# Frequency mixing on one core: applying products in four blocks, with the next unit's first building groups between them

## What is computed

```python
Vf = jnp.fft.rfft(phi, n=n, axis=0)
Uf_p = jnp.fft.rfft(u, n=n, axis=1)
Uf_m = jnp.fft.rfft(u * sgn3, n=n, axis=1)
U_plus = jnp.fft.irfft(Vf[None, :, :, None] * Uf_p[:, :, None, :], n=n, axis=1)[:, :sl]
...
out = jnp.einsum('btkd,k,kde->bte', U_plus, s, Mpp)
out = out + jnp.einsum('btkd,k,kde->bte', U_minus, s, Mpm)
```

## Time and profile before

| | us |
|---|---|
| median of 3 runs | 3256.39 |
| the 3 runs | 3248.46, 3256.39, 3266.70 |
| the profiled execution, device time | 3252.43 |
| its span | 3250.7 |
| TensorE busy in the span | 2596.3 (80%) |
| VectorE busy | 1553.5 (48%) |
| ScalarE busy | 1357.3 (42%) |
| GpSimd busy | 267.9 (8%) |

### The profile page before, as it was taken

One profiled execution on the slowest core, in us unless ns is written; L12 is line 12 of the kernel. 1 busy time (PEld: TensorE's weight loads), 2 busy tenths in 40 slices (PEclk: granted clock), 3 DMA queues, 4 the chain that ended last, 5 costly groups with the idle time before them and its releaser, 6 DMA issues. The chain is left out here.

```text
span 3250.7 us, 88750 instructions
## 1 busy us (share of the span) xinstructions
PE 2596.3 (80%) x36720; PEld 2013.4 (62%) x36720; DVE 1553.5 (48%) x3537; ACT 1357.3 (42%) x2728; POOL 267.9 (8%) x493
## 2 busy tenths in 40 slices
PE   0556999455449999989999999999777865899999
PEld 0336888322148888888888888887337621555555
DVE  6441333332425565656555556566112342376666
ACT  0552433254036555656555656565110263233322
POOL 0102111000100000000000000000111001100000
PEclk9776888777779999999999999999995677799999
DMA  7337555333531111111111111110785200000000
GB/s 202 118 96 134 103 96 101 116 129 118 120 96 40 40 41 39 48 40 40 40 40 40 40 40 40 40 40 21 244 285 199 70 0 12 5 21 21 19 20 27
DMA packets 160531, 242.34 MB, mean 75 GB/s; under 512 B 37072, under 2 KB 114691, under 8 KB 156639
## 3 DMA queue, kind: packets, MB, share of 16 engines
q1 hardware_dynamic: 122137, 115.68, 12.9%
q0 software_dynamic: 34048, 102.83, 11.8%
q10 hardware_dynamic: 3969, 18.31, 1.4%
HBM read 145.48 MB, written 91.27 MB: 73 GB/s over the span
## 5 line engine op out<-in xcount | busy, mean ns | idle before, releaser
L962 DVE COPY spc_g<-spc_pz 128x512 f32<-128x512 f32 x1088 | 670.5, 682 | 450.4 <-PE spc_pz L860 450.4
L940 ACT ACTIVATE spc_g<-spc_pz 128x512 f32<-128x512 f32 x1088 | 587.0, 610 | 346.3 <-PE spc_pz L860 344.6
L860 PE MATMUL spc_pz<-spc_v,spc_as 108*128 108x128 bf16 x8704 | 601.0, 222 | 40.5 <-issue 29.7
L860 PEld LDWEIGHTS spc_pz<-spc_v,spc_as 108*128 108x128 bf16 x8704 | 516.6, 99 | 134.7 <-issue 48.0
L878 PE MATMUL spc_pz<-spc_g,spc_u 128*20 128x128 f32 x17408 | 503.8, 274 | 30.0 <-DVE spc_g L962 18.1
L878 PEld LDWEIGHTS spc_pz<-spc_g,spc_u 128*20 128x20 f32 x17408 | 480.3, 133 | 62.6 <-ACT spc_g L940 41.2
L845 PE MATMUL spc_pu<-spc_f,spc_s 128*128 128x256 f32 x816 | 223.6, 399 | 70.9 <-DMA spc_s<-s_sf 70.9
L1591 DVE SCALAR_TENSOR_TENSOR moe_yt<-moe_ex,moe_gb,moe_yt 128x128 f32<-128x128 f32 x768 | 209.7, 343 | 145.8 <-ACT moe_yt L1495 144.7
L1445 PE MATMUL moe_ex<-moe_ew,moe_d 128*128 128x512 f32 x512 | 253.2, 617 | 17.1 <-DVE moe_yt L1591 17.1
L507 DVE SCALAR_TENSOR_TENSOR inv_xo<-inv_pa,inv_mask,inv_xo 128x256 f32<-128x256 f32 x256 | 123.5, 483 | 228.4 <-PE inv_pa L465 173.3
L485 ACT ACTIVATE inv_b<-inv_pb 112x1024 f32<-112x1024 f32 x128 | 125.5, 1022 | 227.6 <-PE inv_pb L444 227.6
(11 more groups left out here) (188 smaller groups left out, 2509.9 us busy)
## 6 DMA issues: line engine op xcount, KB each, us to landing
s_yd<-spc_yo SPq DMA_DIRECT2D x136, 160.0 KB
spc_s<-s_sf POOLq DMA_DIRECT2D x36, 512.0 KB, 6.5
ivs_y<-s_yd POOLq DMA_DIRECT2D x34, 512.0 KB, 5.4
s_td<-ivs_to SPq DMA_DIRECT2D x34, 512.0 KB, 4.7
s_sf<-fwd_so ACTq DMA_DIRECT2D x16, 1024.0 KB, 5.4
bck_t<-s_td POOLq DMA_DIRECT2D x32, 512.0 KB, 3.8
inv_x<-s_xn SPq DMA_DIRECT2D x88, 112.0 KB
inv_x<-s_xn POOLq DMA_DIRECT2D x88, 112.0 KB, 7.6
```

What stands on the lines that cost most here:

```text
L860: m = pe.matmul(pz[:, (p + 2) % 3, e // 4, 2 * FT * (e % 4):2 * FT * (e % 4) + 2 * FT], AS[:, x, 8 * p + e, :], V[:, k, x, :, FT * t:FT * ...
L940: act.activation(g_out(p, 0), g_in(p, 0), ACT.Copy).then_inc(ga, 1)
L962: v.tensor_copy(g_out(p, 1), g_in(p, 1)).then_inc(gd, 1)
```

## The change

Each unit's order on the three engines is written anew. The sixteen building groups of the next unit are no longer all behind the four blocks of applying: group 0 stands behind block 0, groups 1 and 2 behind block 1, groups 3 and 4 behind block 2, the other eleven behind block 3. The engines that copy follow the same order. For this the tile G gets 168 columns instead of 128 for each frequency (EO = 40 more), and plus units use columns 0 to 127, minus units 40 to 167. The groups are taken in an order (`pair_of`) in which the first five write the forty columns that the other unit doesn't read. All blocks of applying use the two banks of one pair (`y_at`), the building groups the others (`PAIR`), and from group 7 on all three pairs. The second step stands behind groups 5, 10 and 15 of the next unit's building. Tokens, their factors and yo become single buffers; GpSimd loads the first tokens and filters ahead of AS.

The core of the diff (sixteen groups of unit 0 are built ahead of the loop; `copy_g`, `copy_y` and `add_y` hold the same operations as before with their waits):

```diff
-        G = A.sb("g", [P, 2 * FT, C])
+        G = A.sb("g", [P, 2 * FT, C + EO])
-        Ss = A.sb("s", [P, 2, 2, NB, 2 * C])
-        F = A.sb("f", [P, 2, 2, 4, NF2])
-        yo = A.sb("yo", [P, 2, FT // 4, C])
+        Ss = A.sb("s", [P, 2, NB, 2 * C])
+        F = A.sb("f", [P, 2, 4, NF2])
+        yo = A.sb("yo", [P, FT // 4, C])
...
         def y_at(h):
-            return pz[:, h // 2, h % 2]
+            return pz[:, 0, h % 2]
+
+        def pair_of(x, j):
+
+            return j if x == 0 else (j + NPR - OWN) % NPR
...
+            load_tokens(0)
+            load_filters(0, 0)
+            for x in range(2):
+                for g, part in enumerate(A_PARTS):
+                    sp.dma_start(AS[KX * g:KX * g + KX, x].rearrange("k e d -> k (e d)"),
+                                 S["AS"][x, part].rearrange("k e d -> k (e d)")).then_inc(as_in, 16)
+            load_filters(1, 1)
...
                     sp.wait_ge(u_done, UB * (f + 1))
-                    load_tokens((f + 2) % NF1, k)
+                    load_tokens(f + 1)
...
+                        make_y(f, k, t, x, 0)
+                        if more:
+                            if end:
+                                pe.wait_ge(in_v[1 - k], 96 * (i + k) + 96)
+                            make_g(nf, nk, nt, nx, 0)
+                        make_y(f, k, t, x, 1)
+                        if more:
+                            make_g(nf, nk, nt, nx, 1)
+                            make_g(nf, nk, nt, nx, 2)
+                        make_y(f, k, t, x, 2)
+                        if more:
+                            make_g(nf, nk, nt, nx, 3)
+                            make_g(nf, nk, nt, nx, 4)
+                        make_y(f, k, t, x, 3)
+                        if more:
+                            for j in range(OWN, NPR):
+                                make_g(nf, nk, nt, nx, j)
+                                if not last and j in STEPS:
+                                    if t == 0 and x == 0 and j == OWN:
+                                        pe.wait_ge(in_s, 48 * (f + 2))
+                                    second_step(f + 1, 1 - k, 3 * (2 * t + x) + STEPS.index(j))
```

More of the change, by code:

```diff
@@ L772, in spectrum @@
     NPR = C // 8
+    OWN = 5
+    EO = 8 * OWN
     UB = 3 * NB
+    NH = FT // 16
+    PAIR = (2, 1, 2, 1, 2, 1, 2, 0, 1, 2, 0, 1, 2, 0, 1, 2)
+    STEPS = (OWN, 10, NPR - 1)
     with Arena(nc, "spc") as A:
@@ L802, in one, with f_loop @@
             return ap[bass.ds(i, 1)].rearrange(f"{' '.join(names)} -> ({names[0]} {names[1]}) {' '.join(names[2:])}")
+        def f_loop(eng, body):
+            with eng.Fori(0, NF1 // 2) as i:
+                for k in range(2):
+                    body(2 * i + k, k, i, False)
+            body(NF1 - 1, 0, NF1 // 2, True)
         @block.gpsimd
         def _(sp):
[L806 to L809, removed]
             def load_filters(f, k):
@@ L851, in make_g @@
                 n = NUN * f + 2 * t + x
[L852 to L864, removed]
@@ L866, in make_y @@
-            def make_y(f, k, t, x):
-                n = NUN * f + 2 * t + x
[L868 to L880, removed]
@@ L883, in _ @@
+            pe.wait_ge(in_s, 48)
             for unit in range(UB):
                 second_step(0, 0, unit)
+            pe.wait_ge(in_v[0], 96)
             pe.wait_ge(as_in, 16 * 12)
+            for j in range(NPR):
+                make_g(0, 0, 0, 0, j)
             def body(f, k, i, last):
-                pe.wait_ge(in_v[k], 96 * (f // 2) + 96 if isinstance(f, int) else 96 * i + 96)
-                if not last:
-                    pe.wait_ge(in_s[1 - k], 48 * i + 48 + 48 * k)
                 for t in range(NTL):
@@ L892, in body @@
                     for x in range(2):
[L893 to L913, removed]
+                        end = x == 1 and t == NTL - 1
+                        if end:
+                            nf, nk, nt, nx = f + 1, 1 - k, 0, 0
+                        else:
+                            nf, nk, nt, nx = f, k, t + x, 1 - x
+                        more = not (end and last)
@@ L954, in _, with copy_g, add_y, body @@
         def _(v):
-            def body(f, k, last):
+            def copy_g(n, x, j):
+                v.wait_ge(g_done, NPR * n + j + 1)
+                v.tensor_copy(g_out(x, j, 1), g_in(j, 1)).then_inc(gd, 1)
+            def add_y(f, t, h):
+                n = NUN * f + 2 * t + 1
+                v.wait_ge(y_done, NH * n + h + 2)
+                v.wait_ge(ya, NH * (NTL * f + t) + h + 1)
+                y = yo[:, 4 * h:4 * h + 4, :].rearrange("p g e -> p (g e)")
+                v.tensor_tensor(y, y_at(h), y, ALU.add).then_inc(yd, 1)
+            for j in range(NPR):
+                copy_g(0, 0, j)
+            def body(f, k, i, last):
                 for t in range(NTL):
```

157 lines of the change are left out of this document (115 added, 42 removed).

## The result

| | before | after |
|---|---|---|
| median, 12 runs each | 3248.28 us | 3264.10 us |
| lowest and highest | 3238.57 to 3266.70 | 3250.13 to 3280.51 |
| profiled execution | 3252.43 us | 3271.32 us |
| its span | 3250.7 us | 3269.6 us |

The ratio is 1.0052, with a 95% interval from 1.0027 to 1.0077: the changed kernel is slower, by 16 us in the medians and by 19 us in the two profiled executions. The forecast was 33 us. The direction was right, the size twice too large. Of all runs in this document one, of a_block (3331.41 us), was slow as a whole at a lower granted clock, and is left out of its median and ratio.

A forecast was written before the change was run, and what follows sets the result against it. No copy engine bounds the stage on average; only TensorE's waits, at most 1.4 of 18.6 us a unit, can be won. Spacing +34.8, U +7.8, start -10 give +32.6: 3289 us; forecast 3273 to 3308, wider range 3252 to 3314.

The forecast's parts named there:

- Waiting taken away: TensorE's waits for copies in a unit fall from 1.41 to 0.98 us: a gain of 0.43 us.
- Changes of shape: Six new passages a unit between applying and building: 3 x 0.19 us towards building, 3 x 0.15 us back.
- The units of before: Unit length before the change, from one pair: 18.56 and 18.70 us, mean 18.63, against 19.15 after.
- The wait for U: Second step now right before the applying products that need its output: +0.49 us, 16 times, +7.8 us.
- The start: Tokens loaded ahead of AS bring the first applying product from 958.95 to 949.0: -10 us (-6 to -14).
- The last units and the returns: All 67 spacings counted at +0.52 us; seven returns of TensorE's loop taken as unchanged, 0, with 3 us each way.
- Single buffers, row spacing: Single token and result buffers stay hidden by 3 us each; G's rows of 672 B instead of 512 B cost 0.
- B: Rival: a change of shape costs nothing where a group stands between two blocks; unit 18.13 us, 3221 us, chance 0.07.
- C: Rival: only the new direction, building to applying, is free; 30 us less, 3259 us, chance 0.11.
- E: Rival: a single buffer's load or result write is late by 6 us, 3 us shown 16 times; 3337 us, chance 0.09.
- D: Rival: loop returns shrink because filter loads no longer run beside the refill; 28 us less, 3261 us, chance 0.07.
- F: Rival: early groups do not overlap, copies or products slow beside applying; +10, 3299 us; forecast with F 0.66.

The follow-up runs named there:

- a_block: The changed kernel with the five early building groups behind the fourth applying block instead of between the blocks: 3301.82 us, ratio 1.0116 to the kernel before.
- b_unroll: The kernel before with TensorE's hardware loop of the stage written out as straight code: 3196.46 us, ratio 0.9823.
- a_unroll: The changed kernel with TensorE's hardware loop of the stage written out as straight code: 3209.97 us, ratio 0.9858 to the kernel before.
- a_split: The changed kernel with applying blocks 0 and 1 and groups 0 and 1 cut in alternating halves, more shape changes: 3301.87 us, ratio 1.0147 to before.

## Why the prediction was right or wrong

The direction and the mechanism were right. The step that failed is the largest term of the sum, 67 x 0.52 = +34.8 us for the spacing of the units. Measured, it is about +17 us: the 67 spacings grew by 28.9 us, of which 10.8 are the waits for U and 1.3 the returns. Both lengths in that difference were wrong, the unit after by the price of a change of shape, the unit of before by taking one pair for all.

By its own steps, in the two profiled executions (forecast +32.6, measured +18.9 us):

- *Waiting taken away*: right. In the earlier trace rows the run of five waited 0.29 us; the changed kernel's early groups do not wait at all, its two runs of five do as before (2.53 us to the step at 1506.09 for one), and the wait for the last copy is there with 0.27 us idle.
- *Changes of shape*: right in kind, mis-sized. Towards building 0.18 to 0.19 us for 0.19; back 0.10 us for 0.15, in the terms of the sum, from the start of one run to the start of the next. A round trip costs 0.29 us and not 0.34; the 0.37 of the inverse stage, with other shapes, did not carry over. The unit became 19.00 instead of 19.15: -10 us. By the rule that was weighed, the Trainium skill's (TensorEngine Tiling (Array Packing), Key Properties) drain at each change of tiling mode, the forecast would have been 0.19 for the change back, further off. The trace agrees that both directions cost something (0.15 and 0.14 us by the starts of single products); that it is a drain, no run shows.
- *The units of before*: one pair of units stood for all. The third unit of most f takes 19.03 us and not 18.56, 8 us over the stage, which the change does not pay there; it pays 3 us in the first units of the odd f. Net -5 us. b_unroll shows that the long third units belong to TensorE's loop, a_unroll that the long first ones of the changed kernel do. The third units were in the trace of before and were not read; one of them, with 7.65 us of applying and not 7.19:

```profile
1071.88 7.72 PE L878 MATMUL spc_pz<-spc_g,spc_u 128*20 128x128 f32 x256 [0.21 <-DVE spc_g L962]
1079.53 2.70 PE L860 MATMUL spc_pz<-spc_v,spc_as 108*128 108x128 bf16 x40
```

- *The wait for U*: right in kind, 0.7 for 0.49 us, +3 us. a_unroll has 0.38: part of it, 0.3 us, is there only with the loop. It is 0.19 us from the step to the products (1.91 for 1.72), and in five of nine units as much again in the run behind group 5. Why is not settled.
- *The start*: 10.8 us for 10, 9.2 of them its own.
- *The last units and the returns*: three units at the end were counted at +0.52 each; with no steps in them and a stall of before gone they gave 1 us back, -2.5 us. Returns cost 54 us before and 55 after, as taken.
- *Single buffers, row spacing*: hidden and free, as taken.

These add up to 32.6 - 10 - 5 + 3 - 1 - 2.5 + 1 = 18 us, of 18.9. The two errors in the unit lengths, of about 0.1 us each, had the same sign, so that they did not cancel, and the factor of 67 made 15 us of them. The rivals: free passages (B) and free in one direction (C) are out by a_split, late single buffers (E) by the waits of the kernel after, shorter returns (D) by the sum of the returns. F, copies slowed beside applying products, is there (701 against 682 ns) and no early group or block waits for them. The bound given for B, below 0.04 us for a passage, does not follow from its bracket: (0.43 - 0.12) / 6 to (0.57 - 0.12) / 6 is 0.05 to 0.075 us. The 0.14 measured is above both.

## What to carry to other kernels

Interleaving two kinds of products pays a fee for each change of the array's shape, so count the passages before the waits: here six new ones cost 0.87 us in a unit to save some 0.45 of waiting. Where an engine waits in bursts for a copy that keeps up on the average, first spread out the work already there, in pieces that share its shape. And before a difference of two unit lengths is multiplied by 67, take both lengths from all units of the trace.

## What the runs showed of the hardware that was not expected

- A round trip from 128-column weights to four 20-column ones side by side and back cost 0.29 us: between the starts of runs 0.10 us into the narrow shape and 0.18 to 0.19 out of it, whatever the number of products between (4 to 16 building products, 16 to 128 applying ones).
- A return of TensorE's loop cost 7.7 us on the average, part of it at a granted clock of 0.50, and loop code had short stalls elsewhere too; writing the loop out took 1.8% off the whole kernel.
- VectorE's copies to G slowed from 682 to 701 ns in the mean when five of sixteen ran beside applying products (700 to 773 ns for these five), and two of ScalarE's five went from 597 to 789 and 804 ns. With rows of 672 B instead of 512 B, and no applying beside them, VectorE's copies did not slow (683 ns).
